# One wait for two exponentials in a state-space scan, and a load moved from ACT's to SP's DMA queue

## What is computed

```python
delta = softplus(einsum('blr,er->ble', dt_low, W_dt) + b_dt)
A = -exp(A_log)
def step(h, inp):                 # over the 2048 tokens
    d_t, B_t, C_t, x_t = inp
    dA = exp(d_t[..., None] * A)
    dBx = d_t[..., None] * B_t[:, None, :] * x_t[..., None]
    h = h * dA + dBx
    y = sum(h * C_t[:, None, :], axis=-1)
y = (y + xc * D_param) * silu(z)
out = einsum('ble,de->bld', y, W_out) + b_out
```

## Time and profile before

| | us |
|---|---|
| median of 2 timed runs | 5613.83 (5610.61 to 5617.05) |
| the profiled execution | 5553.08 |
| its span, slowest core (4) | 5551.4 |
| busy: PE, DVE, ACT, POOL | 2761.2, 2548.1, 1754.7, 501.4 |
| scans on DVE (1024) | 1342.6 |
| exponentials `m_dA` on ACT (1024) | 731.9 |

### The profile page before, as it was taken

How to read it: one execution, slowest core, us unless ns; L and a number is a source line. 1 busy time by engine, 2 the same in 40 slices (tenths; PEclk the granted TensorE clock), 3 DMA queues, 4 the chain that set the end, 5 groups by cost and what they waited for, 6 DMA issues and landing times.

```text
span 5551.4 us, 41788 instructions; the slowest of 8 cores (5519.6 to 5551.4 us)
## 1 busy us (share of the span) xinstructions
PE 2761.2 (50%) x12960; PEld 1204.9 (22%) x12960; DVE 2548.1 (46%) x2198; ACT 1754.7 (32%) x2562; POOL 501.4 (9%) x570
## 2 busy tenths in 40 slices
PE   3452333423333233342222323798896444498998
PEld 3221111101111011110010112233332222233333
DVE  0108999169994499972999500001101333110010
ACT  2314555035552255530555223211111222212110
POOL 1140111101112011110000010100000000100000
PEclk9786666756766666776565755898997666688988
DMA  7432000510004200014000275422224111322221
GB/s 124 103 48 36 19 19 17 86 50 20 19 19 48 88 17 20 21 22 100 9 15 12 66 144 137 135 86 71 79 76 90 62 57 61 135 67 92 88 72 57
DMA packets 185919, 345.41 MB, mean 62 GB/s; under 512 B 49924, under 2 KB 70532, under 8 KB 184676
## 3 DMA queue, kind: packets, MB, share of 16 engines
q1 hardware_dynamic: 137126, 247.51, 14.3%
q0 software_dynamic: 39360, 86.84, 10.0%
q10 hardware_dynamic: 9216, 8.39, 0.5%
HBM read 301.06 MB, written 71.45 MB: 67 GB/s over the span
## 4 chain that ended last, share of the span: by engine, by line
PE 33%; DVE 28%; DMA 13%; issue 11%; DVEq 8%; ACT 4%; POOL 1%; another core or an unknown queue 1%; SPq 0%; ACTq 0%; POOLq 0%
DVE m_hall L57 15%; PE f_pAa L57 11%; PE f_pAb L57 11%; DVEq L73 8%; DVE m_dBall L57 5%; PE a_pA L57 3%; PE m_pB L57 3%; DMA m_yfr<-s_yfc 3%; DVE m_txd L57 2%; DMA p_wnat<-W 1%; DMA m_wouta<-s_WoutT 1%; PE m_pA L57 1%; POOL m_diag L57 1%; DMA s_x<-xres 1%; DMA xres<-x 1%
## 5 line engine op out<-in xcount | busy, mean ns | idle before, releaser
L57 DVE TENSOR_TENSOR_SCAN m_hall<-m_dA,carry,m_dBall 128x512 bf16<-128x512 f32 x1024 | 1342.6, 1386 | 11.3 <-issue 10.2
L57 PE MATMUL m_pB<-m_gall,eye 128*128 128x512 bf16 x1024 | 362.1, 531 | 1436.3 <-DVE m_gall L57 1436.3
L57 ACT ACTIVATE m_dA<-m_delta,A_fm 128x512 f32<-128x512 f32 x1024 | 731.9, 721 | 954.0 <-DVE m_hall L57 852.9
L57 DVE BATCH_NORM_STATS2 stat<-xres 128x6 f32<-128x512 f32 x128 | 82.0, 683 | 1003.6 <-DMA xres<-s_x 817.0
L57 PEld LDWEIGHTS m_pB<-m_gall,eye 128*128 128x128 bf16 x1024 | 126.7, 128 | 1660.4 <-issue 1630.1
L57 ACT ACT_TABLE_LOAD x158 | 202.7, 1283 | 632.7 <-DVE r1a L57 298.8
L57 DVE TENSOR_TENSOR xres<-xres,b_bc 128x1024 f32<-128x1024 f32 x32 | 39.2, 1225 | 760.1 <-PE f_pAb L57 383.7
L57 POOL TENSOR_TENSOR m_diag<-convw_fm,eye 128x1920 bf16<-128x1920 f32 x64 | 239.7, 3745 | 1416.5 <-PE m_pB L57 1416.4
L57 DVE TENSOR_TENSOR m_dBall<-m_dxb,m_bcB 128x8192 bf16<-128x8192 bf16 x64 | 283.2, 4425 | 5.9
L57 DVE TENSOR_TENSOR m_gall<-m_hall,m_bcC 128x8192 bf16<-128x8192 bf16 x64 | 283.2, 4425 | 0.3 <-issue 0.3
L57 PE MATMUL f_pAa<-f_xna,f_w1a 128*128 128x512 bf16 x1024 | 255.4, 394 | 17.9 <-DMA f_w1a<-s_W1T 17.9
(11 more groups left out here) (157 smaller groups left out, 3465.4 us busy)
## 6 DMA issues: line engine op xcount, KB each, us to landing
xres<-s_x SPq DMA_DIRECT2D x96, 512.0 KB, 3.3
f_w1a<-s_W1T SPq DMA_DIRECT2D x128, 256.0 KB, 2.7
f_w1b<-s_W1T SPq DMA_DIRECT2D x128, 256.0 KB, 2.7
s_x<-xres SPq DMA_DIRECT2D x48, 512.0 KB
xres<-x SPq DMA_DIRECT2D x32, 512.0 KB, 3.9
m_wz<-s_WinT POOLq DMA_DIRECT2D x64, 256.0 KB, 2.9
m_wzz<-s_WinT SPq DMA_DIRECT2D x64, 256.0 KB, 2.8
m_wouta<-s_WoutT SPq DMA_DIRECT2D x64, 256.0 KB, 3.0
```

The costliest lines, as they stand in the source:

```text
L57: box["i"] = getattr(e, fname)(*a, **kw)
```

## The change

Two things. In `scan`, the sixteen exponentials and scans of a chunk are issued in eight pairs: both exponentials of a pair, of which only the second raises `s_dA`; one wait of DVE; then both scans. The exponential of half 0 still waits for all scans but the latest issued (`s_sc.n - 1`), that of half 1 now waits for all scans issued so far (`s_sc.n`), which is again the scan two states back. `dAb` stays at two halves. In `wout`, `yfr` is loaded by SP, behind `woutt`, and ACT's waits for it go.

```diff
-                    for n in range(16):
-                        nn = n % 2
-                        gidx = c * 16 + n
-                        ac.wait(s_dl)
-                        if gidx >= 2:
-                            ac.wait(s_sc, s_sc.n - 1)
-                        ac.activation(out=dAb[:, nn, :], in_=delta[:, sl, :], func=AF.Exp,
-                                      scale=A_fm[:, c, n:n + 1]).inc(s_dA, 1)
+                    for p in range(8):
+                        for half in range(2):
+                            n = p * 2 + half
+                            gidx = c * 16 + n
+                            ac.wait(s_dl)
+                            if gidx >= 2:
+                                ac.wait(s_sc, s_sc.n - 1 + half)
+                            tok = ac.activation(out=dAb[:, half, :], in_=delta[:, sl, :],
+                                                func=AF.Exp, scale=A_fm[:, c, n:n + 1])
+                        tok.inc(s_dA, 1)
                         ve.wait(s_dA)
-                        ve.tensor_tensor_scan(out=hall[:, n, :], data0=dAb[:, nn, :],
-                                              data1=dBxall[:, n, :],
-                                              initial=carry[:, gidx % 256:gidx % 256 + 1],
-                                              op0=ALU.mult, op1=ALU.add).inc(s_sc, 1)
+                        for half in range(2):
+                            n = p * 2 + half
+                            gidx = c * 16 + n
+                            ve.tensor_tensor_scan(out=hall[:, n, :], data0=dAb[:, half, :],
+                                                  data1=dBxall[:, n, :],
+                                                  initial=carry[:, gidx % 256:gidx % 256 + 1],
+                                                  op0=ALU.mult, op1=ALU.add).inc(s_sc, 1)
...
-                ac.wait(l_yfd0, l_yfd0.n); ac.wait(l_yfd1, l_yfd1.n)
                 for k in range(16):
...
-                        ac.wait(sem, v)
...
-                    ac.dma_start(out=yfr[:, ksl, :], in_=s_yfc[k, :, :]).inc(s_wzp[ksl], 16)
+                    sy.dma_start(out=yfr[:, ksl, :], in_=s_yfc[k, :, :]).inc(s_wzp[ksl], 16)
```

## The result

The changed kernel is slower: 6051.28 us, median of 12 runs (6001.94 to 6160.7), against 5583.61 us for the kernel before in 10 runs (5556.27 to 5674.72). The ratio is 1.0783, 95% interval 1.0733 to 1.0834, which is 5583.61 x 0.0783 = 437 us, 409 to 466. Slower by over 2% was forecast; the prediction's ratio was 6105 / 5613.83 = 1.087.

What follows compares the result with a forecast made beforehand. The prediction took no engine to bound the whole kernel, but DVE to bound the scan stage. Its terms, +488 - 8 + 12 = +492 us, added to the median 5613.83, gave 6105 us, range 6020 to 6175.

Steps and rivals of the forecast that it cites:

- The bound and the mechanism: Scan loop: DVE bounds it and stands at each pair border for the half-1 exponential, 448 times.
- The border, 1.09 us (term +488): Scan loop: each of 448 pair borders costs two hand-overs and one exponential, 1.09 us; +488 us, bounds 448 to 515.
- One of the signs named for the profile after: Profile after, scan loop: the busy time of scans and exponentials was to stay unchanged.
- POOL in the gaps (term -8): Scan loop, quarters 0 to 2: POOL's `m_diag` work partly falls into a chunk's first gap; -8 us, bounds 0 and -38.
- The projection (term +12): Output projection: `yfr` issued behind `woutt` on SP costs 0.47 us a round; +12 us in all.
- The two-sided bound for the stretch under the broadcasts: Output projection during POOL's 32 broadcasts: one queue in place of two, taken as 0, bounds +36 and -20 us.
- The dropped waits (0): Scan loop: 512 of 1024 waits go and save nothing; taken as 0, bound 15 us.
- The base: Whole kernel: the added 492 us was put on the timed runs' median, 5613.83 us.
- A: Rival, scan loop: both exponentials of a pair fall behind scan 2p-1, 278 us more, 6385 us; chance 0.02.
- B: Rival, scan loop: dropped waits make scans start sooner and give the time back, about 5700 us; chance 0.02.
- C: Rival, output projection: one queue under the broadcasts loses 36 us (6141) or wins 20 (6085); chance 0.12.
- D: Rival, scan loop: POOL hides the whole -38 us in the gaps in place of -8, 6075 us; chance 0.09.

Runs made afterwards that it cites:

- scan_only: Changed kernel with the `yfr` load back on ACT's queue, so only the scan pairs differ from the kernel before; ratio 1.0768 (1.0651 to 1.0885).
- pair_ring4: Changed kernel with `dAb` at four halves, each exponential waiting for the scan four states back; ratio to the kernel before 0.9981 (0.9923 to 1.0039).
- batch4_ring4: `pair_ring4` with batches of four exponentials and four scans; 192 waits, scan stage +193.5 us; total 5925.55 us gives no ratio.
- half_exp: Changed kernel with the half-1 exponential over 256 of 512 columns; DVE's wait for `m_dA` 411.6 to 316.7 us, scan stage 2439.1 us.
- the two kernels without `diag`: Kernel before and changed kernel, each with POOL building `diag` only in quarter 0; scan stages 1949.9 and 2408.2 us.

## Why the prediction was right, and where it was off

*The bound and the mechanism:* right. DVE bounds the scan stage, the second exponential of a pair waits for the scan that holds its buffer, and 448 borders are the added time, each one exponential, two hand-overs and the lost overlap of two scans. `scan_only` puts it in the loop, `pair_ring4` gives the exponentials a free half and takes away the time, `batch4_ring4` scales it with the number of borders, `half_exp` with the length of the exponential.

*The border, 1.09 us (term +488):* too large; the two kernels without `diag` give 458 for 448, 1.02 each, and quarter 3 gives (602.6 - 486.8) / 112 = 1.03. Of the parts, the start of the second exponential at 2.55 and its 0.72 came out to the hundredth. The way from ACT to DVE was taken as 0.17 from the earlier trace rows and is 0.11. In that row DVE stands at the start of a quarter, where the code gives it two waits in a row (`s_sp`, then `lg`); at a pair border it is one. That the second wait is the difference wasn't tried. That is 0.06 x 448 = 27 of the 30 us by which the term was over. For the same reason the chunks of quarter 3 are 38.47 us apart (median) in place of 38.9. One of the signs named for the profile after was wrong: the scans' busy time isn't unchanged, it has the 25.0 us of lost overlap and POOL's saving in it.

*POOL in the gaps (term -8):* right in kind, too small: -21 by the two kernels without `diag`. I had spread POOL's 42 starts evenly over 2.2 to 4.2 us. In the changed kernel most of them gather in one place: on core 4, 29 of the 42 lie between 2.64 and 2.70 us after the first scan, in the gap. Three more start at 2.33 or 2.34, in the pair's second scan; they wait for its end, and so the whole gap is theirs (these chunks are 2.15 us longer than without `diag`, where the 29 are 2.5 longer), which my count left out. What holds the 29 together is PE's work before POOL: each start follows, one for one, the length of the sum over the states (correlation 0.97). PE is idle before that sum (28.9 us ahead of the one at 1732.54), and inside it the granted clock goes from 0.50 (1.2 GHz; 1734 to 1735 us) to 1.00 (2.4 GHz; from 1736 on). On core 4 the sum took 5.00 to 5.05 us in 32 of the 42 chunks; in `half_exp` it took 4.9 to 6.5, and the starts are spread with it (correlation 0.99). What sets the moment at which the clock rises stays open, so that the 29 meet the gap is chance: core 0 of the same execution has its starts spread up to 5.3 us and none of them between 2.64 and 2.70. By rule of the Trainium skill (SBUF — State Buffer, "SBUF: two separate sides"), whoever starts first holds the shared ports to the end of its instruction; the timeline agrees on both sides, with POOL's multiply ending 3.19 us after the scan that was running, and the scans then stopped, 2.50 us in place of 3.10 where 0.69 us of POOL's work lay in the gap.

*The projection (term +12):* about 8 by the ten traces. Quarters 0 to 2 lose 9 where 8 was forecast, but that their cause is the issue time isn't shown; quarter 3 was to lose 3.8 (46 us in place of 42) and wins 1, since the issue does come later on SP, but the landing takes 2.7 us in place of 3.2. The Trainium skill (DMA: Bandwidth & Descriptors, "Issuing engines are not separate DMA queues") gives the second issuer's gain as its issue time alone; in quarter 3 even that was not lost. The two-sided bound for the stretch under the broadcasts was not needed: neither end came.

*The dropped waits (0):* right, by `pair_ring4`.

*The sum:* 458 - 21 + 8 = 445 from the measured terms against 437 from the ratio (409 to 466) and 432 on core 4; of the forecast's 492 the borders have 30 too much, POOL's term 13, the projection 4.

*The base:* I put the sum on the median of two runs, 5613.83. With ten runs the median is 5583.61, and that of the changed kernel 6051.28. On that base the forecast would have been 6076. Some luck is in how near 6105 came, 54 us over: the base was 30 too high and the sum 55, but the two medians lie 31 further apart than the ratio says. From the ratio alone the time is 5583.61 + 437 = 6021, just above the lower end of the range, 6020.

*The rivals:* A (both exponentials in the gap) would have made gaps of 1.6 us; they are 0.92. B and C fell as told. D, all of POOL hidden (-38), was nearer than its chance of 0.09 says: a little over half of that.

## What to carry to other kernels

A buffer of two halves overlaps two engines only while they take turns one item at a time. Work on a batch as large as the buffer, with one wait for the batch, and the last item of each batch lies bare: here one exponential of 0.72 us, two hand-overs and a lost overlap, 1.03 us for each border, though ACT was busy for only about half of the scan stage. Before grouping signals count the slots: here twice the batch was tried and cost nothing, but grouping gained nothing either, since here a wait that was met cost nothing that shows.

When the same instruction has a longer mean where another engine works beside it, look whether that engine stops it: in the scans' mean of 1386 ns lay the 3.1 us that POOL took from a chunk, and moving that work to the DMA queues gave 2.8%.

## What the runs showed of the hardware

- A satisfied semaphore wait on DVE costs nothing that shows: sixteen scans in 18.92 us with sixteen waits, 18.91 with eight.
- From the end of an ACT instruction to the start of a DVE instruction that waits for it: 0.11 us; both ways together 0.20 us, the same with an exponential of 0.72 and of 0.51 us.
- The exponential of 128 x 512 float32 takes 0.721 us, of 128 x 256 0.506: halving the columns takes off 30%.
- A GpSimd multiply of 128 x 1920 stops the DVE scans for 3.10 us, wherever in a scan it starts. It waits for the running scan itself: it ends 3.19 us after that scan's end (39 of 42), and its recorded length goes from 3.38 to 4.46 us with the time to that end. If it starts in a gap of DVE, the stop is shorter (2.50 us with 0.69 in the gap).
- The same 128 KB load lands in 3.2 us from ACT's queue and 2.7 us from SP's (medians of 16), beside a 256 KB load that SP issued just before; that one lands 0.3 to 0.5 us sooner too (medians of 64, all ten traces).
